# The last layer's matrix 64 bytes ahead of a 512-byte line, and the first layer's two banks signalled one by one, in a float32 feed-forward and spectral-mixing kernel

## The reference, cut to what matters

```python
x = x + 0.5 * ffn(layernorm(x))
x = x + gelu(fft_convolution(layernorm(x))) @ W.T + b
x = x + 0.5 * ffn(layernorm(x))

def ffn(x):                                   # 256 -> 1024 -> 1024 -> 1024 -> 256, ternary weights
    h = silu(x @ w1.T * w1_s) * (x @ w2.T * w2_s)
    h = gelu(h @ h1.T * h1_s)
    h = gelu(h @ h2.T * h2_s)
    return h @ w3.T * w3_s
```

## Time and profile before

| | before |
|---|---|
| median of 3 runs | 1441.88 us (1441.57 to 1443.68) |
| profiled execution | 1441.73 us, span 1439.9 us |
| TensorE matmul busy | 1432.2 us, 99% of the span, 6918 records |
| TensorE weight loads busy | 1162.6 us, 81% |
| VectorE busy | 986.7 us, 69% |
| ScalarE busy | 476.6 us, 33% |
| GpSimd busy | 48.3 us, 3% |

### The profile page before, as it was taken

How to read it: one execution, slowest core, us unless ns; L and a number is a source line. 1 busy time by engine, 2 the same in 40 slices (tenths; PEclk the granted TensorE clock), 3 DMA queues, 4 the chain that set the end, 5 groups by cost and what they waited for, 6 DMA issues and landing times.

```text
span 1439.9 us, 17283 instructions
## 1 busy us (share of the span) xinstructions
PE 1432.2 (99%) x6918; PEld 1162.6 (81%) x6918; DVE 986.7 (69%) x1736; ACT 476.6 (33%) x724; POOL 48.3 (3%) x42
## 2 busy tenths in 40 slices
PE   9999999999999999999999999999999999999999
PEld 4788888888778878788787878878878788888887
DVE  7867867675778887848878587784777754353433
ACT  5524342433324223233242232422424223141331
POOL 0000000000000000010000100001000010000000
PEclk9999999999999999999999999999999999999999
DMA  9000000012113221031210312012120112010000
GB/s 366 16 0 30 30 30 30 16 45 59 41 55 136 67 66 59 25 119 44 88 59 12 132 45 73 30 44 99 59 74 15 59 41 74 1 36 9 30 1 16
DMA packets 53906, 80.28 MB, mean 56 GB/s; under 512 B 2752, under 2 KB 45632, under 8 KB 52544
## 3 DMA queue, kind: packets, MB, share of 16 engines
q1 hardware_dynamic: 53824, 79.15, 16.2%
HBM read 57.12 MB, written 22.02 MB: 55 GB/s over the span
## 4 chain that ended last, share of the span: by engine, by line
PE 97%; DVE 2%; ACT 0%; issue 0%; POOL 0%; DVEq 0%
PE ps L1317 80%; PE ps L1391 8%; PE ps L1442 3%; PE ps L1495 2%; PE ps L1293 1%; PE ps L1436 1%; PE ps L1437 1%; PE ps L1404 1%; PE ps L1485 0%; DVE low L1176 0%; PE ps L1310 0%; DVE hid_b_lo L1211 0%; PE ps L1419 0%; PE ps L1427 0%; DVE hid_b_hi L1209 0%
## 5 line engine op out<-in xcount | busy, mean ns | idle before, releaser
L494 ACT ACTIVATE act_o<-ps,scales 128x512 f32<-128x512 f32 x384 | 264.6, 690 | 911.9 <-PE ps L1317 909.7
L1317 PE MATMUL ps<-hid_b_hi,h 128*128 128x512 f32 x1024 | 401.5, 392 | 0.5 <-DVE hid_b_lo L1211 0.5
L1317 PE MATMUL ps<-hid_b_lo,h 128*128 128x512 f32 x1024 | 398.7, 389 | 0.0
L1317 PE MATMUL ps<-hid_a_hi,h 128*128 128x512 f32 x992 | 391.0, 394 | 0.2
L1317 PE MATMUL ps<-hid_a_lo,h 128*128 128x512 f32 x992 | 386.4, 390 | 0.0
L1317 PEld LDWEIGHTS ps<-hid_b_hi,h 128*128 128x128 f32 x1024 | 192.2, 188 | 42.2 <-issue 1.2
L1317 PEld LDWEIGHTS ps<-hid_b_lo,h 128*128 128x128 f32 x1024 | 192.2, 188 | 40.7 <-issue 1.2
L1317 PEld LDWEIGHTS ps<-hid_a_hi,h 128*128 128x128 f32 x992 | 186.2, 188 | 45.7 <-DVE hid_a_lo L1202 2.4
L1317 PEld LDWEIGHTS ps<-hid_a_lo,h 128*128 128x128 f32 x992 | 186.2, 188 | 39.8 <-issue 2.2
L1317 PE MATMUL ps<-hid_b_hi,w 128*128 128x512 f32 x480 | 189.5, 395 | 0.0
L1317 PE MATMUL ps<-hid_b_lo,w 128*128 128x512 f32 x480 | 188.1, 392 | 0.0
(11 more groups left out here) (268 smaller groups left out, 1269.5 us busy)
## 6 DMA issues: line engine op xcount, KB each, us to landing
ks<-k_d SPq DMA_DIRECT2D x32, 512.0 KB, 3.9
raws<-in_weights SPq DMA_DIRECT2D x10, 1024.0 KB, 15.6
xin<-in_x SPq DMA_DIRECT2D x8, 512.0 KB, 3.9
x_d<-xin SPq DMA_DIRECT2D x8, 512.0 KB, 2.8
z_d<-xin SPq DMA_DIRECT2D x8, 512.0 KB, 2.8
zb<-z_d SPq DMA_DIRECT2D x8, 512.0 KB, 4.7
wb<-x_d SPq DMA_DIRECT2D x8, 512.0 KB, 4.1
x_d<-wb SPq DMA_DIRECT2D x8, 512.0 KB, 3.3
```

The source lines that it names most:

```text
L494: A(act_o[:, k % ACT_SLOTS], bank(source), func, scale=scale).then_inc(s_act, 1)
L1317: last = MM(o, weight[:, k, cols].bitcast(dt), part[:, k].bitcast(dt), start=(k == 0 and i == 0), stop=(k == n - 1 and i == len(act_) - 1))
```

## The change

It has two parts. **Addresses:** `w3` leaves the end of the weights and is laid ahead of them, so that it begins 64 bytes before a multiple of 512; `flag` and `expo` fill the 64 bytes behind it, and `w1`, `w2`, `h1`, `h2` and everything after begin on 512-byte lines as before. **Signals of the first layer:** the tensor engine raises a new semaphore, `s_half`, after the product with `w1`, and the scalar engine's SiLU waits for that instead of `s_u`. The vector engine's `gate` waits for `s_u` beside `s_act`. The tensor engine waits for `s_act` of `m - 2` before the product with `w1`, and for `s_gate` of `m - 2` only before the product with `w2`.

```diff
-        shapes = (("w1", [P, KD, HID]), ("w2", [P, KD, HID]), ("h1", [P, KH, HID]), ("h2", [P, KH, HID]),
-                  ("w3", [P, KH, D]))
-        scales, small, single, flag, expo, FRONT = zone(
-            0, ("scales", [P, 4, KH]), ("small", [P, N_SMALL]), ("single", [P, 4]), ("flag", [P, 1], I32),
-            ("expo", [P, J]))
-        FRONT += -(base + FRONT) % LINE
-        w1, w2, h1, h2, w3, W0 = zone(FRONT, *((n, s, F32R) for n, s in shapes))
-        raws, _ = zone(FRONT, ("raws", [P, WEIGHTS]))
+        scales, small, single, LAST = zone(0, ("scales", [P, 4, KH]), ("small", [P, N_SMALL]), ("single", [P, 4]))
+        LAST += (LINE - 64 - base - LAST) % LINE
+        w3, FRONT = zone(LAST, ("w3", [P, KH, D], F32R))
+        raw_3, _ = zone(LAST, ("raw_3", [P, KH * D]))
+        flag, expo, FRONT = zone(FRONT, ("flag", [P, 1], I32), ("expo", [P, J]))
+        assert (base + FRONT) % LINE == 0
+        w1, w2, h1, h2, W0 = zone(FRONT, ("w1", [P, KD, HID], F32R), ("w2", [P, KD, HID], F32R),
+                                  ("h1", [P, KH, HID], F32R), ("h2", [P, KH, HID], F32R))
+        raws, _ = zone(FRONT, ("raws", [P, WEIGHTS - KH * D]))
...
+        def raw(c):
+            return raws[:, chunk(c)] if c < N_CHUNKS - 1 else raw_3[:, :]
...
             def hidden(T, k, func, scale):
-                act.wait_ge(s_u, at_u(T, k))
+                if k < KH:
+                    act.wait_ge(s_half, at_gate(T, k))
+                else:
+                    act.wait_ge(s_u, at_u(T, k))
...
             def gate(T, m):
                 dve.wait_ge(s_act, at_u(T, m))
+                dve.wait_ge(s_u, at_u(T, m))
...
                 else:
-                    pe.wait_ge(s_gate, at_gate(T, m - 2))
+                    pe.wait_ge(s_act, at_u(T, m - 2))
...
-                product(bank(o), w1 if T else first(0), cols, z_parts, KD, dt)
+                product(bank(o), w1 if T else first(0), cols, z_parts, KD, dt).then_inc(s_half, 1)
+                if m >= 2:
+                    pe.wait_ge(s_gate, at_gate(T, m - 2))
                 product(bank(o + 1), w2 if T else first(1), cols, z_parts, KD, dt).then_inc(s_u, 1)
```

More of the change, by code:

```diff
@@ L252, in build @@
         s_bn, s_mv, s_stat, s_rstd, s_z, s_z2 = (sem(n) for n in ("s_bn", "s_mv", "s_stat", "s_rstd", "s_z", "s_z2"))
+        s_half = sem("s_half")
         s_zt, s_zhi, s_zlo, s_u, s_act, s_gate, s_ghi, s_glo, s_hi, s_split, s_o, s_upd, s_x = (sem(n) for n in (
@@ L297, in load_weights @@
                 for c in range(first, last):
-                    sp.dma_start(raws[:, chunk(c)], a["weights"][:, chunk(c)]).then_inc(s_w[c], 16)
+                    sp.dma_start(raw(c), a["weights"][:, chunk(c)]).then_inc(s_w[c], 16)
             by_columns = lambda t: t[:, 0:2 * CHUNK].rearrange("p (k n) -> p k n", n=HID)
@@ L627, in round_weights @@
                 act.wait_ge(s_low, max(c, 1))
-                A(place(c), raws[:, chunk(c)], ACT.Copy).then_inc(s_placed, 1)
+                A(place(c), raw(c), ACT.Copy).then_inc(s_placed, 1)
             act.wait_ge(s_one, 1)
@@ L1170, in check_weights @@
                     dve.wait_ge(s_w[c], 16)
-                words = raws[:, chunk(c)].bitcast(I32)
+                words = raw(c).bitcast(I32)
                 if c == 1:
-                    V.tensor_tensor(low[:, :], raws[:, chunk(0)].bitcast(I32), words, ALU.bitwise_or).then_inc(s_low, 1)
+                    V.tensor_tensor(low[:, :], raw(0).bitcast(I32), words, ALU.bitwise_or).then_inc(s_low, 1)
                 else:
@@ L1333, in layer_one @@
                 else:
-                    pe.wait_ge(s_gate, at_gate(T, m - 2))
+                    pe.wait_ge(s_act, at_u(T, m - 2))
                 cols, o = slice(m * P, (m + 1) * P), 2 * (m % 2)
                 z_parts = (zhi, zlo) if T else (zf[:, :, :],)
-                first = lambda c: raws[:, chunk(c)].rearrange("p (k n) -> p k n", k=KD)
-                product(bank(o), w1 if T else first(0), cols, z_parts, KD, dt)
+                first = lambda c: raw(c).rearrange("p (k n) -> p k n", k=KD)
+                product(bank(o), w1 if T else first(0), cols, z_parts, KD, dt).then_inc(s_half, 1)
+                if m >= 2:
+                    pe.wait_ge(s_gate, at_gate(T, m - 2))
                 product(bank(o + 1), w2 if T else first(1), cols, z_parts, KD, dt).then_inc(s_u, 1)
```

## The result

The change takes the kernel from 1441.79 us (median of 6 runs, 1441.27 to 1443.68) to 1431.34 us (6 runs, 1430.93 to 1433.32): a ratio of 0.9928, 95% interval 0.9915 to 0.9941. That is 10.4 us less; forecast were 1429.5 us and a range of 1424 to 1438.5.

What follows compares the result with a forecast made beforehand. TensorE, busy 99% of the span, was taken to bound the kernel. Gains of 7.1 + 3.9 + 1.4 = 12.4 us gave 1429.5 us against 1441.88, range 1424 to 1438.4 (chance 0.57 that both parts work).

Steps and rivals of the forecast that it cites:

- Part 2, tile 0: New signals in tile 0: last SiLU and its queue move up, TensorE's 1.13 us pause goes; 1.4 us gained, bounds 0.5 and 1.6.
- Part 2, tiles 1 to 15: New signals in the other tiles: TensorE's waits for `gate` and the last `hid_a_lo` go; 3.9 us gained, bounds 3 and 4.5.
- the surplus of a piece: Time of a piece of first and hidden layers over 226.9 ns a matmul: 0.30 us average over 14 pieces, 4.5 us in all.
- the 0.2 us kept for waits that are not caught: Tiles 1 to 15: 0.2 us of the 4.5 us left out for waits the new signals would not remove.
- The 0.4 us for settling: Start of the first layer, tiles 1 to 15: slower first distances that stay, 15 x 0.03 us, taken off the 4.5 us.
- Part 1: New address of `w3`, last layer alone: 1008 matmul distances shrink by 7 ns each, 7.1 us gained.
- the 113 ns: Last layer: expected distance between matmuls after moving `w3`, against 120 ns now; 1008 x 7 ns gained.
- the floor of 108.5: Last layer: lowest possible distance in ns between matmuls, 11.5 less than now; 11.6 us gained at most.
- The prediction's own sign of being wrong: Wrong if the last layer's distance is above 118 or below 108 ns, or pauses turn up before the product with `w2`.
- Rival 1: Last layer: surplus is a fixed price of swapping F32R weights, only the signals gain; 1436.6 us, chance 0.26.
- Rival 2: Last layer: the offset collides worse, 130 ns a matmul, 10 us lost against 5.3 gained; 1446.6 us, chance 0.05.
- Rivals 3 and 4: 3: offset costs a little, signals hide it, 1438 to 1442 us, chance 0.07. 4: signals fail, pauses stay, 1434.8 us, 0.05.

Runs made afterwards that it cites:

- signals alone: The kernel before with only the lines on `s_half`, `s_act`, `s_u` and `s_gate` changed, `w3` where it was: 1434.64 us against 1441.15.
- the address alone: The kernel after with the signals' lines as before, so only `w3` moved: 1437.39 us against 1441.15, ratio 0.9974.
- the map: Versions of the kernel after with `w1`, `w2`, `h1`, `h2` or `w3` at other places against a 512-byte line: 1431.87 to 1465.17 us, one execution each.

## Why the prediction was right

**Part 2, tile 0: right, 1.4 us forecast, 1.7 measured.** The queue behind the last SiLU moved as worked out: `hid_a_hi` of step 7 was expected at 38.4 and came at 38.67 in an execution that began 0.4 later; the pause of 1.13 us went, the flag came earlier, and the tile hung on VectorE until the piece of 114. The step stands.

**Part 2, tiles 1 to 15: right in kind, a quarter too small: 3.9 forecast, 5.2 measured** (signals alone: first layers 3.6 us, hidden layers 1.6). The term that was mis-sized is the surplus of a piece, 0.30 us on average, and three things went into that. I measured it against 226.9 ns, a distance that I had from a piece of pure hidden layer, which holds some settling itself; against the settled 226.7 ns the 2960 matmuls of the 14 pieces hold up to 0.6 us more. Tile 4 is not among the 14: its wait of 0.53 us for `hid_a_lo` breaks its piece in two, it was counted as an average tile, worth 0.26 us (3.9 / 15), and it gained 0.67. And the 0.2 us kept for waits that are not caught was not needed. The 0.4 us for settling was right: with the signals alone the first layers still start 26 or 27 ns over in 13 of 15 tiles.

**Part 1: right in kind and in sign, half the size: 7.1 us forecast, 3.2 measured** in the last layers' starts (3.8 us by the medians with the address alone, the starts of the first layers included). The failed term is the 113 ns that I took in the middle between 117.5 and the floor of 108.5. Six of 16 stages do stand at 113.3; the other ten stand at 117.8, which is the row that I had called nearest. Nothing came near the floor at any offset: it was drawn from the 0.11 us that one weight load holds back the next and from float32 transposes, and the lowest settled distance of F32R matmuls of 256 columns in all 14 kernels is 113.3.

The prediction's own sign of being wrong, a distance above 118 ns, is met by the mean of all distances of the last layer (119.5), though not by its settled steps.

With both parts in, tiles 1 to 15 gain 5.4 us ahead of their last layers (3.8 and 1.6), as the first layers also start more settled. So the misses are 3.9 us too much, 1.5 and 0.3 too little: 2.1 us between the 12.4 forecast and the 10.3 found. That the total came so close is in part luck, as misses of opposite sign met. The range says little of part 1: without it the kernel takes 1434.64 us, which also lies inside.

**The rivals.** Rival 1 (the offset does nothing) fell with the address alone. It leaned on what the Trainium skill states in "TensorE: Matmul & The Clock Gate", "Step-by-step: what each phase is for": two independent read ports, so that loading the next weights takes no bandwidth from the running matmul. What was drawn from that, that an offset can do nothing, does not agree with these traces: 64 bytes of one operand against the other move the distance from 120.0 to 117.8 or 113.3 ns, and for 512 columns from 226.7 to 233.4. Whether it is bandwidth that the two reads share is not shown. Rival 2, the collision that gets worse, did not come in the last layer, but it is just what 512 columns show. Rivals 3 and 4 did not come: both parts gained, each by itself.

That the surplus depends on how two reads stand against each other was argued from the settling in the earlier trace rows. The runs show that it depends on the difference of the two operands' places; that it is their reads which collide, and in what, is argued and not shown. That the effect repeats every 256 bytes is measured at 0 and 256 and at 192 and 448 for both lengths, and at 64 and 320 for 512 columns, where the same two steps appear; the other rows of the map take it as given.

## What to carry to other kernels

Where TensorE is always busy, read the distance between the starts of matmuls, not their durations, and compare it before and after a pause: distances that settle elsewhere say that there is something to move. The place of a tensor modulo 256 bytes against the block that is loaded beside it is worth trying on a single layer of a kernel like this one, and has to be measured for each length of the stream by itself: what helped 256 columns cost 512 columns 3%. Where TensorE waits on another engine's result, ask which buffer is free first, and signal that one by itself; then look at what else is queued behind the engine that waits for the signal, as the largest gain of any tile, 1.7 us, came from such a queue in tile 0.

## What the hardware showed that I had not expected

In these kernels F32R matmuls with a 128 x 128 weight load each run in one of a few steps and mostly stay in it until a pause: 120.0, 118.7, 118.3, 117.8, 117.3, 116.7 or 113.3 ns for 256 columns. The offset decides which steps there are; which of them a stage takes at the same offset is open. The settling at the start of the first layers, 26 or 27 ns over in most tiles before, depends on the last layer ahead of them too: it came down to between 0 and 22 ns with the change, but with `w3` at 288, where the last layer is at 116.7 ns in most tiles, it is 10 to 50 ns. The float32 matmuls of tile 0, which the profile shows as two records each, did not change: 429 ns a record in all 14 kernels, though their blocks stood in six different places against a 512-byte line.
